# A layer of linear attention and ternary FFN on eight cores: the order of SP's loads in the first FFN tiles, two more down units measured in attention, numerators stored as whole rows, context parts in three banks

## The reference, cut to what matters

```python
# x: (4, 4096, 1024) f32, 16 heads of 64, FFN inner size 4096
n = layernorm(x)
q = softmax((n @ Wq.T + bq) @ Wfq.T + bfq, axis=-1)   # over all 1024
k = softmax((n @ Wk.T + bk) @ Wfk.T + bfk, axis=-1)
v = n @ Wv.T + bv
scores = einsum('bhsd,bhtd->bhst', q, k)              # no softmax over t
ctx = einsum('bhst,bhtd->bhsd', scores / scores.sum(-1), v)
x = x + ctx
# BitLinear: tokens rounded to 8 bits by their row maximum, weights to
# -1, 0, 1 by the mean of |w| over the whole matrix
n = layernorm(x)
h = silu(bit(n, w_gate)) * bit(n, w_up)               # inner 4096
y = x + bit(h, w_down)
```

## Time and profile before

| | |
|---|---|
| median of 3 runs | 1139.72 us (1138.64 to 1140.58) |
| the profiled execution's own time | 1136.21 us |
| its span on the slowest core (core 0) | 1134.7 us |
| spans of the other cores | 1122.8 to 1133.7 us |
| busy on core 0: PE, DVE, ACT, POOL | 1065.9, 624.1, 490.2, 204.2 us |
| mean DMA rate of core 0 | 176 GB/s |

### The profile page before, as it was taken

How to read it: one execution, slowest core, us unless ns; L and a number is a source line. 1 busy time by engine, 2 the same in 40 slices (tenths; PEclk the granted TensorE clock), 3 DMA queues, 4 the chain that set the end, 5 groups by cost and what they waited for, 6 DMA issues and landing times.

```text
span 1134.7 us, 13520 instructions; the slowest of 8 cores (1122.8 to 1134.7 us)
## 1 busy us (share of the span) xinstructions
PE 1065.9 (94%) x5414; PEld 499.8 (44%) x5414; DVE 624.1 (55%) x1140; ACT 490.2 (43%) x604; POOL 204.2 (18%) x132
## 2 busy tenths in 40 slices
PE   5859899999989989897799999999999999999998
PEld 2324454554445544343344444444444444444443
DVE  3356555667657677665644744744644644744311
ACT  2226876678777856475622222222222222222110
POOL 0000000024334330264421021021021021011010
PEclk9979999999989999999899999999999999999999
DMA  9969999789999976787851351341341351341340
GB/s 267 294 197 337 344 327 330 248 275 323 328 312 326 295 225 196 167 234 251 213 121 38 84 121 38 85 121 38 84 121 38 84 121 38 84 94 39 55 111 38
DMA packets 201262, 199.65 MB, mean 176 GB/s; under 512 B 170096, under 2 KB 170096, under 8 KB 193008
## 3 DMA queue, kind: packets, MB, share of 16 engines
q1 hardware_dynamic: 184560, 194.61, 58.5%
q10 hardware_dynamic: 16640, 4.20, 1.6%
HBM read 148.45 MB, written 29.36 MB: 157 GB/s over the span
## 4 chain that ended last, share of the span: by engine, by line
PE 75%; DMA 8%; DVE 7%; ACT 6%; issue 2%; POOL 1%; SPq 1%; ACTq 1%; DVEq 0%
PE ps L558 33%; PE ps L538 19%; PE ps L410 19%; DMA stage<-wfkT 2%; DMA wst<-wgT 2%; DMA wst<-wdT 2%; DMA bvb<-bv 2%; ACT wg L346 1%; DVE nm L738 1%; DVE lg L734 1%; PE ps L459 1%; SPq L232 1%; ACT wd L346 1%; PE ps L448 1%; ACT eq L1077 1%
## 5 line engine op out<-in xcount | busy, mean ns | idle before, releaser
L558 PE MATMUL ps<-wg,aqT 128*128 128x512 fp8e4 x1024 | 244.8, 382 | 2.0 <-DVE aqT L964 2.0
L558 PE MATMUL ps<-wu,aqT 128*128 128x512 fp8e4 x1024 | 242.8, 380 | 0.2
L1120 ACT ACTIVATE silu<-ps,l 128x512 f32<-128x512 f32 x128 | 87.5, 685 | 318.4 <-PE ps L558 314.2
L997 DVE SCALAR_TENSOR_TENSOR hmid<-ps,l,silu 128x512 f32<-128x512 f32 x128 | 95.8, 749 | 145.7 <-PE ps L558 109.4
L324 POOL TENSOR_SCALAR wst<-wst,msum 128x2048 f32<-128x2048 f32 x48 | 96.0, 2002 | 380.1 <-DMA wst<-wgT 280.8
L558 PEld LDWEIGHTS ps<-wu,aqT 128*128 128x128 bf16 x1024 | 100.1, 98 | 122.6 <-DVE hmid L997 1.8
L558 PEld LDWEIGHTS ps<-wg,aqT 128*128 128x128 bf16 x1024 | 99.0, 99 | 113.9 <-issue 3.4
L410 PE MATMUL ps<-wck,xT 128*128 128x512 bf16 x512 | 122.3, 394 | 20.6 <-DVE xT L729 12.7
L1168 POOL TENSOR_SCALAR hmid<-hmid,hsc 128x1024 f32<-128x1024 f32 x64 | 70.6, 1122 | 313.5 <-DVE hsc L1018 313.5
L410 PE MATMUL ps<-wv,xT 128*128 128x512 bf16 x512 | 117.4, 383 | 3.9 <-DVE rz L769 3.9
L989 DVE SCALAR_TENSOR_TENSOR xr<-ps,hsc,xr 128x512 f32<-128x512 f32 x32 | 24.0, 751 | 172.4 <-PE ps L538 172.4
(11 more groups left out here) (95 smaller groups left out, 1055.7 us busy)
## 6 DMA issues: line engine op xcount, KB each, us to landing
wst<-wgT SPq DMA_DIRECT2D x32, 1024.0 KB, 11.4
wst<-wuT SPq DMA_DIRECT2D x32, 1024.0 KB, 8.7
wst<-wdT SPq DMA_DIRECT2D x32, 1024.0 KB, 7.3
xr<-x_own SPq DMA_DIRECT2D x32, 512.0 KB, 6.6
s_hq<-hqs SPq DMA_DIRECT2D x32, 512.0 KB, 4.1
xr<-x_oth SPq DMA_DIRECT2D x16, 512.0 KB, 12.7
y<-xr SPq DMA_DIRECT2D x16, 512.0 KB, 3.3
stage<-wk SPq DMA_DIRECT2D x8, 512.0 KB, 10.1
```

Source lines behind the costliest of these rows:

```text
L558: pe(lambda e, c=c: e.matmul(out, a[:, c * 128:c * 128 + 128], w8[:, c * DI + 512 * oc:c * DI + 512 * oc + 512], start=(c == 0), stop=(c = ...
L997: dv(lambda e: e.scalar_tensor_tensor(hmid[:, 512 * oc:512 * oc + 512], U[oc % 2], l2[:, s + 6:s + 7], sl, op0=ALU.mult, op1=ALU.mult), [a ...
L1120: ac(lambda e: e.activation(silu[:, (oc % 2) * 512:(oc % 2) * 512 + 512], G[oc % 2], ACTF.Silu, bias=0.0, scale=l2[:, s + 5:s + 6]), [at(" ...
```

## The change

1. `units`: ten units of w_down's pass 1 stand among the own ones of attention, after every three others, instead of eight after every four. NA grows from 72 to 74. The last unit of attention is now the last of w_up.
2. `ffn_units`: the 22 units that are left go to tiles 0 to 3 as 6, 5, 5 and 6, each at a named column group. The second mean (`mean_dv1`, `mean_pe`, `mean_dv2`) moves from oc 3 to oc 1 of tile 1.
3. SP: for each t, eld of t+2, two unit loads, the stores of tile t-1's products, the other unit loads, the transposed loads of tile t-1's products, then output store and x load. Before, the moves of tile t's own products closed its turn.
4. The context parts of tiles 1 to 3 go to KB[0], KB[1] and KB[2] and all follow oc 0 on PE, with no wait for DVE between them. From tile 4 on it is as before. DVE's order of them stays.
5. `s_eq` is stored as 128 rows of 1024 per tile, and each tile comes back by eight DMA transposes of 128x128 instead of one.

```diff
+NP1 = 10
...
-    for u in range(8):
-        own[5 * u + 4:5 * u + 4] = [(1, 2, u)]
+    for u in range(NP1):
+        own[4 * u + 3:4 * u + 3] = [(1, 2, u)]
...
-    units += [(1, 2, u) for u in range(8, 16)] + [(2, 2, u) for u in range(16)]
+    units += [(1, 2, u) for u in range(NP1, 16)] + [(2, 2, u) for u in range(16)]
...
+    for t, at_oc in enumerate([(1, 2, 3, 4, 5, 6), (3, 4, 5, 6, 7),
+                               (2, 3, 4, 6, 7), (2, 3, 4, 5, 6, 7)]):
+        ffn_units[t] = {oc: n1 + k for k, oc in enumerate(at_oc)}
+        n1 += len(at_oc)
...
-                at("y", t - 1, h) if t else at("cm", 0, 1 + h)],
+                at("y", t - 1, h) if t else at("cm", LAG, 1 + h)],
...
-    CB = [KB[0], T, KB[0]]
+    def ctx_bank(t, part):
+        return KB[part] if t <= LAG else (KB[0], T, KB[0])[part]
...
-            if t == 1 and oc == 3:
+            if t == 1 and oc == 1:
                 mean_pe(2, t_free[0])
...
-                pe_ctx(t + 1, 0, CB[0], at("cm", t, 2))
-                pe_ctx(t + 1, 1, CB[1], t_free[0])
-                t_free[0] = at("cm", t + 1, 1)
-            if t + 1 < TQ and oc == 1:
-                pe_ctx(t + 1, 2, CB[2], at("cm", t + 1, 0))
+                pe_ctx(t + 1, 0, ctx_bank(t + 1, 0), at("cm", t, 2))
+                if t + 1 <= LAG:
+                    pe_ctx(t + 1, 1, KB[1], None)
+                    pe_ctx(t + 1, 2, KB[2], None)
+                else:
+                    pe_ctx(t + 1, 1, T, t_free[0])
+                    t_free[0] = at("cm", t + 1, 1)
+            if LAG < t + 1 < TQ and oc == 1:
+                pe_ctx(t + 1, 2, KB[0], at("cm", t + 1, 0))
...
-        spt(f"dL{t % 2}", eld[t % 2][...], s_eq.ap()[t * D:(t + 1) * D, :],
-            [at("eqs", t), free], ("eld", t))
+        for c in range(CH):
+            spt(f"dL{t % 2}", eld[t % 2][:, c * 128:c * 128 + 128],
+                s_eq.ap()[t * 128:(t + 1) * 128, c * 128:c * 128 + 128],
+                [at("eqs", t), free] if c == 0 else (),
+                ("eld", t) if c == CH - 1 else None)
...
-        for n in ffn_units.get(t, []):
-            if n + NWF < len(units):
-                unit_load(n + NWF)
-        for h in range(2):
-            move_hq(t, h)
-        for h in range(2):
-            load_hq(t, h)
-        if t >= LAG:
-            store_y(t - LAG)
+        loads = [n + NWF for n in ffn_units.get(t, {}).values()
+                 if n + NWF < len(units)]
+        for n in loads[:2]:
+            unit_load(n)
+        if t:
+            hq_out(t - 1)
+        for n in loads[2:]:
+            unit_load(n)
+        if t:
+            hq_back(t - 1)
+        if t > LAG:
+            store_y(t - 1 - LAG)
...
-        acd(f"dE{k}", s_eq.ap()[t * D:(t + 1) * D, :].rearrange(
-            "(c n) k -> n c k", n=128),
-            eqs[k][...].rearrange("p (c k) -> p c k", k=128),
+        acd(f"dE{k}", s_eq.ap()[t * 128:(t + 1) * 128, :], eqs[k][...],
             [at("EQ", t)], ("eqs", t))
```

More of the change, by code:

```diff
@@ L109, in build_nc @@
     y_out = nc.dram_tensor("y", [NQ, D], F32, kind="ExternalOutput")
-    s_eq = nc.dram_tensor("s_eq", [TQ * D, 128], BF16, kind="Internal")
+    s_eq = nc.dram_tensor("s_eq", [NQ, D], BF16, kind="Internal")
     s_hq = nc.dram_tensor("s_hq", [2 * DI, 128], BF16, kind="Internal")
@@ L380, in build_nc @@
         n0 += k
[L381 to L384, removed]
+    ffn_units = {}
+    n1 = NA
+    for t, at_oc in enumerate([(1, 2, 3, 4, 5, 6), (3, 4, 5, 6, 7),
+                               (2, 3, 4, 6, 7), (2, 3, 4, 5, 6, 7)]):
+        ffn_units[t] = {oc: n1 + k for k, oc in enumerate(at_oc)}
+        n1 += len(at_oc)
+    assert n1 == len(units)
     unit_slot = {n: i for i, l in slot_units.items() for n in l}
@@ L652, in store_y, with hq_out, hq_back @@
            [at("y", t, 0), at("y", t, 1)], ("yst", t))
+    def hq_out(t):
+        for h in range(2):
+            move_hq(t, h)
+    def hq_back(t):
+        for h in range(2):
+            load_hq(t, h)
     def move_hq(t, h):
@@ L670, in load_hq @@
             [at("eqs", TQ - 1 - k) for k in range(NEQ)], ("hqT", t, h))
-    late_units = [n for t in range(4) for n in ffn_units[t]]
     load_eld(0)
-    for n in late_units[:NWF]:
+    for n in range(NA, NA + NWF):
         unit_load(n)
@@ L681, in build_nc @@
             load_eld(t + 2)
-        for n in ffn_units.get(t, []):
-            if n + NWF < len(units):
-                unit_load(n + NWF)
-        for h in range(2):
-            move_hq(t, h)
-        for h in range(2):
-            load_hq(t, h)
-        if t >= LAG:
-            store_y(t - LAG)
-        if NXF <= t + 3 < TQ:
-            load_xf(t + 3)
-    for t in range(TQ - LAG, TQ):
+        loads = [n + NWF for n in ffn_units.get(t, {}).values()
[10 more added lines that the diff above has]
+            store_y(t - 1 - LAG)
+        if NXF <= t + 2 < TQ:
+            load_xf(t + 2)
+    hq_out(TQ - 1)
+    hq_back(TQ - 1)
+    for t in range(TQ - 1 - LAG, TQ):
         store_y(t)
@@ L1028, in build_nc @@
                 if oc == 0:
-                    dv_ctx(t + 1, 0, CB[0])
-                    dv_ctx(t + 1, 1, CB[1])
+                    dv_ctx(t + 1, 0, ctx_bank(t + 1, 0))
+                    dv_ctx(t + 1, 1, ctx_bank(t + 1, 1))
                 if oc == 1:
-                    dv_ctx(t + 1, 2, CB[2])
+                    dv_ctx(t + 1, 2, ctx_bank(t + 1, 2))
                 if oc == 2:
@@ L1137, in build_nc @@
     for t in range(TQ):
-        us = ffn_units.get(t, [])
+        us = ffn_units.get(t, {})
         early = 0 < t <= LAG
@@ L1152, in build_nc @@
                 ac_aq(t + 1)
-            if oc and us[oc - 1:oc]:
-                unit_ac(us[oc - 1])
+            if oc in us:
+                unit_ac(us[oc])
         if t >= LAG:
@@ L1182, in build_nc @@
             gp_xb(t + 2)
-        for n in ffn_units.get(t, []):
+        for n in ffn_units.get(t, {}).values():
             unit_gp(n)
```

## The result

The changed kernel is slower, by 0.65%: 1146.72 us median (1144.4 to 1148.53, 5 runs), beside 1139.71 of the kernel before on the same chip; the ratio is 1.0065, with a 95% interval of 1.0045 to 1.0085. I had forecast 1126.1, faster. The slowest core's span is 1142.9 us (core 6; the others 1132.8 to 1142.5), against 1134.7.

What follows compares the result with a forecast made beforehand. PE, busy 94% of the span, was taken as the bound, with its waits in tiles 0 to 3 to win. FFN 12.6 us plus attention 1 gave 13.6 less: 1126.1 us median, range 1117 to 1134.

Steps and rivals of the forecast that it cites:

- the sum: FFN gain: 0.9 us over tiles 0 and 1, 6.2 in tile 2, 5.5 before the first down product, 12.6 in all.
- The mean's matmul: Tile 1, oc 1: DVE's list lets it start 13.4 us into the tile; PE's wait grows from 3.7 to 6 us or more.
- DVE does not hold tiles 2 and 3: Rival, chance 0.13: those tiles come near 28.5 us, the gain to 19 or 20, the time to about 1119.
- Eight transposes for one: SP's eld loads: 0.8 us a piece, 6.4 us of SP per tile; nothing late up to 1.4 us a piece, price zero.
- the small transposes cost their overhead one by one: Rival, chance 0.08: beyond 1.5 us a piece, eld and units come late, 24 us for each further us of a piece.
- Order of SP's loads: Tiles 2 and 3: unit loads issued when their slots are free, so `aq`'s unit wait goes; 6.2 and 5.5 us won.
- the row at 510.55: Tile 2 of the old profile: a unit's load issued only then, since moves of tile 1's products closed SP's list ahead.
- The two terms: Attention: freed DMA and ACT hold from whole rows against two more units nearly cancel; taken as -1 us, between -6 and +7.
- Three banks: Context parts: tile 0's wait of 1.63 us goes; removing those in tiles 1 to 3 is worth nothing by itself.

Runs made afterwards that it cites:

- one_piece: Changed kernel with numerators again stored as 1024 rows of 128 and one transposed load per tile; ratio 0.9946 to the kernel before.
- four_pieces: `rows_one` with each eld brought back by four transposes of 256 rows instead of one; ratio 0.9992 to the kernel before.
- order_old: `one_piece` with SP's list in the order of the kernel before; ratio 0.9951 to the kernel before.
- ten_units: Kernel before with ten units in attention, 5, 5, 6, 6 in tiles 0 to 3, second mean at oc 1; ratio 1.0025 to the kernel before.
- rows_only: Kernel before with only numerators stored as whole rows and eight transposes a tile; ratio 1.0158 to the kernel before.
- rows_one: Changed kernel, whole rows kept, each eld brought back by one transpose in memory order, PE reading weights with stride 8; ratio 0.9939 to the kernel before.
- banks_old: `one_piece` with the context parts in the banks and places of the kernel before; ratio 0.9959 to the kernel before.
- rows_all_mean: `rows_one` with the second mean asked for at tile 1's start and FFN products also stored as whole rows; ratio 0.9905 to the kernel before.

## Why the prediction was wrong

**Tiles 0 to 2 went by the sum.** The mean's matmul was forecast 43.0 us after the first G and came after 42.7; its wait 6 to 7 us, measured 6.5. Tile 2 starts 67.1 us after the first G (forecast 65.9; the clock loss behind the mean was some 1.0 larger, 6.55 us for two groups of 1.89 each), and takes 31.2 us as forecast, held by DVE: `aq` waits 1.1. The rival "DVE does not hold tiles 2 and 3" fell.

**The step that failed** is the one under "Eight transposes for one": "up to 1.4 us a piece nothing is late, both ends included", and with it the price zero. Two sizes in it were wrong. A piece costs 1.23 us, near the upper end, since an issue costs the same for 128 rows as for 1024: 11.2 us a tile where I put 6.4. Worse, I took the moves of products as they are in the kernel before, where the last unit load has been issued 6 to 10 us ahead of them: 3.4 us for the stores, 6.1 for the transposed loads. Right behind unit loads of 1 MB they took 7.0 and 12.2 (medians of the eight cores). So on core 6 SP was busy with the moves and the pieces until 25.6 us into tile 2, where its next unit load had to go at about 20 by my own reckoning; in `one_piece` (core 0) that load went 16.8 us into the tile. In tile 3 the last unit load went after 40.9 us, where I had 21. Together SP's turn was 37.5 us, more than a tile, and what I had priced at zero cost 14.2 us (`one_piece`), or 1.8 to 2.0 us a piece (`four_pieces`). That is more than the 8.7 us that the other parts took off. My rival "the small transposes cost their overhead one by one" had the right mechanism, with a chance of 0.08 and a threshold of 1.5 us that isn't there: pieces of 1.2 us cost time from the first three on.

The Trainium skill, "DMA: Bandwidth & Descriptors", Rules for kernel authors, which I weighed and set aside, advised to join small transfers, and it was right here. Its 2.0 us of fixed cost sits mostly in completion by its own account, and that account is of DMAs issued by GpSimd, not by SP. The rows here show a cost of another kind: each piece held SP for 1.23 us (median from issue to landing: 2.5 us), and it is the issues that line up.

**Order of SP's loads.** The waits for `aq` fell as forecast, but not by the edit that I named. I credited the order of the loads, by the row at 510.55; `order_old` shows no gain from the order, so the number came true by another part than the one I named, most likely the spread of the units. That part of the forecast came true by luck.

**The rest of the sum.** Without the pieces, parts 1 to 4 took 8.7 us off the first tiles, not 12.6. On core 0 of `one_piece` it was 9.8: tile 3 starts 97.5 us after the first G (forecast 97.1), and down starts 36.45 us later, where I had 34.15. `aq` started 27.5 us into the tile instead of 26.1, and ACT then waited 0.8 us for the last unit, whose load went 24.9 us into the tile instead of 21. Why the other cores won less was not traced.

**Attention.** The two terms cancel, as said: +4.3 us for two units (`ten_units`), -1.7 (`rows_only`) and -3.0 to -3.7 (`rows_one` and the changed kernel against `one_piece`) for whole rows; 0.7 longer in all, where I had -1. The long ACT issues did vanish.

**Three banks** were worth the 1.6 us of tile 0 (2.0 in `banks_old`), as said.

In sum: the mean span of the eight cores grew by 8.0 us in the profiled executions (the ratio gives 7.4 for the slowest core): first tiles +5.5, attention +0.7, and +1.8 in the first down product, which runs at a lower clock behind its long wait. That last term stood nowhere in the forecast. It goes with the wait of down: in `one_piece`, where down waits 2.5 to 5.1 us, the product still took 15.5 us or more on seven cores of eight.

## What to carry to other kernels

A queue's issue time is a budget of its own: add up every issue of one turn, at its duration in the crowd that it will stand in, and compare it with the length of the turn after the change, not before. Here a transposed load cost its issue per instruction, 1.2 to 1.3 us from 128 to 1024 rows, so change the layout in memory or the stride of the reader rather than cut it up. And before crediting a reordering, ask which of the edits made together removed the wait.

## What the runs showed of the hardware

- A transposed load's issue on SP: 1.23 us median at 128 rows, 1.21 at 256, 1.23 to 1.30 at 1024, 2.1 to 2.2 at 2048 rows (`hqTa`, `hqTb` of the changed kernel).
- The same issue behind unit loads in flight: up to 10.0 us for 2048 rows in the changed kernel. Two of them took 12.2 us right behind three unit loads, 6.3 in the old order (medians of eight cores, changed kernel and `order_old`).
- A store of 2048 pieces of 256 bytes on SP: 0.38 us in the first tiles of the kernel before, 6.5 to 8.5 at most on each core of the changed kernel, right behind unit loads. Stored as rows of 4 KB, at most 0.9 us in the same place (`rows_all_mean`).
- Weight loads read with a stride of 8 or 16 bf16 elements: 145 and 144 ns instead of 98. Matmuls beside them did not take longer: 226 ns instead of 221 (128x130) and 379 as before (128x512).
- The store of 128 rows of 2 KB on ACT: 0.34 us median and at most 0.39 on all eight cores of six kernels; as 1024 pieces 0.38 median, the longest 1.8 to 6.9 us on 54 of the 56 cores of seven kernels.
- The 64 matmuls of the first down product, up to the next G: 13.8 us on seven cores before, after waits of 1.1 to 2.4 us; 15.4 to 16.6 on all eight cores of the changed kernel, after waits of 14 to 18 us. The granted clock in one of them was 0.89, before 1.00.
